# Layer 2's graph attention in one pass over the edges, and linear attention in a phase of its own

## The chip, the cores and the metric

The kernel runs on one core of one Trainium2 chip. Its time is the device time of one execution in microseconds; lower is better. Engines are named as in the profile: PE is TensorE's matrix multiplications and PEld its weight loads, DVE is VectorE, ACT is ScalarE, POOL is GpSimd, SP is SyncE. SPq and ACTq are the queues from which those engines issue transfers.

## What is computed

A graph network with four layers over 3125 nodes of 256 features and 53125 edges, sorted by target. Each layer adds a graph part, a mixing part and a feed-forward part to `x`. The change touches the graph part and the mixing part of layer 2:

```python
# _L2_gnn_ref, 8 heads of 32
h_prime = (x @ W + b).reshape(n, K, F_OUT)
h_src = jnp.sum(h_prime * a_src, axis=2)
h_trg = jnp.sum(h_prime * a_trg, axis=2)
e = jax.nn.leaky_relu(h_src[src] + h_trg[trg], negative_slope=0.2)
e = e - jnp.max(e)                      # one maximum over all edges and heads
exp_e = jnp.exp(e)
denom = jax.ops.segment_sum(exp_e, trg, num_segments=n)
alpha = exp_e / (denom[trg] + 1e-10)
out = jax.ops.segment_sum(h_prime[src] * alpha[:, :, None], trg, num_segments=n)
...
x = x + _L2_gnn_ref(xn, ...) + _L2_mix_ref(xn[None], ...)[0]    # the mixing part is linear attention
```

Each node also has a loop edge to itself, which the kernel handles apart, as `own`.

## The kernel before

The program is a sequence of phases. Each has its own buffers and semaphores and ends with a barrier of all engines. Nodes lie in 25 tiles of 125 rows. Edges are cut into 440 steps of 128 (`STEPS`, `W`), so that all edges of a step have their targets in one tile, whose number stands in `step_tile`; steps with fewer edges are padded. Eight steps are a group (`GROUP`), and there are 55 groups. `StepTiles` loads the tile numbers of a group into registers of an engine.

Layer 2 runs as follows. `project` writes the transformed rows to a table in memory, and `g2_logit` the source logits beside them, 264 columns in all. `start_rows` adds a bias to `x`. Then comes `linear_attention` (phase `m2_att`), with `LogitGather` beside it in the same phase: GpSimd gathers the rows of each step's sources from the table into one of 8 slots (L3562), and SyncE stores the features of each into a second table, `kept2`, and the logits into `alpha` (L3569, L3570). After its own part of the attention, VectorE compares the local target numbers of a group with the partition number (L3590, called `compare` there and `mark` after the change), TensorE multiplies this matrix with the target logits of the step's tile, 8 columns wide, to expand them to the edges (L3603), and ScalarE copies the result (L3613). Each product of a step shows as two entries of PE in the trace.

Phase `g2_exp` adds both logits for all 440 steps at once, applies the leaky ReLU, masks padded edges (`gone`), finds the one maximum by way of a diagonal matrix that TensorE multiplies with ones (the spread), and takes the exponential. Phase `g2_sp` is `weighted_sums`: SyncE loads the stored rows again into 24 slots; for each pair of steps VectorE scales the rows by `alpha` (`scale`, L3204); for each group it makes the matrix of targets (`compare`, L3196, called `match` after the change); TensorE multiplies the two for each step into one of 8 banks (L3188); and VectorE adds the bank to its tile of `total` (`add`, L3211), each add waiting for the one before. `g2_fin` divides by the denominators and adds to `x`, in four passes over all nodes.

Layer 0 has a loop of the same kind (`gathered_sums`, L829 to L877), in which the sums read gathered rows directly.

The order on each engine is the order of the source: nothing is moved by a compiler, and an engine that waits holds up all that stands behind.

## Time and profile before

| | us |
|---|---|
| median of 3 runs (lowest, highest) | 7098.52 (7088.64, 7107.34) |
| the profiled execution | 7097.57 |
| its span in the profile | 7095.8 |
| PE busy | 4572.0 (64%) |
| PEld busy | 3074.1 (43%) |
| DVE busy | 3424.4 (48%) |
| POOL busy | 2538.9 (36%) |
| ACT busy | 1013.3 (14%) |

The span runs from the first to the last instruction of one profiled execution. Busy shares are means over the whole span, in which stages with different limits follow one another. The mean granted clock of TensorE was 0.752 of full speed; 0.50 is its low level, 1.2 GHz, and 1.00 its high one, 2.4 GHz.

### The profile page before, as it was taken

How to read it: one execution, taken by the hardware profiler on the slowest of the kernel's cores; microseconds unless marked ns; L12 is line 12 of the kernel's file. 1: busy time of each engine (PE TensorE's matmuls, PEld its weight loads, DVE VectorE, ACT ScalarE, POOL GpSimd, SP SyncE). 2: the span in 40 equal slices, each digit the busy share in tenths (PEclk: the TensorE clock that was granted, in tenths of full speed). 3: DMA queues.
4: the chain of work that ended last, by engine and by line, in shares of the span. 5: the costliest groups of instructions: out<-in, count | busy, mean ns of one | idle time of the engine just before them, and what ended most of it. 6: DMA issues, size and time to landing. Idle time of an engine off the chain costs nothing. (4 is left out here: it accounts for less than half of the span.)

```text
span 7095.8 us, 70899 instructions
## 1 busy us (share of the span) xinstructions
PE 4572.0 (64%) x17628; PEld 3074.1 (43%) x17628; DVE 3424.4 (48%) x6656; ACT 1013.3 (14%) x2336; POOL 2538.9 (36%) x2523
## 2 busy tenths in 40 slices
PE   0577768876946886564419436834649996777643
PEld 0245533335833332333218323832426774555533
DVE  6234455550035776896631335207972224677622
ACT  0122200012210000110113100001113332111111
POOL 2455567741014775000130327670000003766333
PEclk9877765558976555897659767558979997988766
DMA  2100023340106998442022238884430002322333
GB/s 83 46 2 2 2 76 98 98 119 25 36 27 217 340 339 256 141 149 68 5 90 74 59 99 215 234 218 136 147 95 1 0 0 71 91 82 77 73 86 101
DMA packets 607539, 722.98 MB, mean 102 GB/s; under 512 B 172860, under 2 KB 504495, under 8 KB 606818
## 3 DMA queue, kind: packets, MB, share of 16 engines
q0 software_dynamic: 144448, 324.12, 16.6%
q1 hardware_dynamic: 440918, 356.52, 16.1%
q10 hardware_dynamic: 21854, 38.57, 1.6%
q8 instruction: 140, 2.29, 0.1%
q14 instruction: 179, 1.47, 0.1%
HBM read 532.77 MB, written 184.69 MB: 101 GB/s over the span
## 5 line engine op out<-in xcount | busy, mean ns | idle before, releaser
L829 POOL DMA_INDIRECT m_rows<-support,far_at x440 | 463.8, 1054 | 1400.4 <-POOLq L96 1164.8
L3188 PE MATMUL g_sp_bank<-g_sp_rows,g_sp_same 128*125 128x260 f32 (+1 forms) x1760 | 530.6, 432 | 276.6 <-DVE g_sp_rows L3204 233.9
L840 PE MATMUL g_sums_bank<-g_sums_rows,g_sums_same 128*125 128x256 f32 x880 | 489.7, 667 | 111.1 <-DMA g_sums_rows<-h,far_at 62.8
L487 POOL DMA_INDIRECT records<-record,place_at x416 | 417.7, 1004 | 353.5 <-issue 116.1
L2945 POOL DMA_INDIRECT g_sc_rows<-keyval,src_at x440 | 423.4, 962 | 322.9 <-POOLq L96 172.6
L3188 PEld LDWEIGHTS g_sp_bank<-g_sp_rows,g_sp_same 128*125 128x125 f32 x1760 | 319.3, 200 | 488.2 <-DVE g_sp_rows L3204 339.3
L829 POOL DMA_INDIRECT g_sums_rows<-h,far_at x440 | 455.1, 1034 | 149.6 <-issue 103.7
L3562 POOL DMA_INDIRECT m_att_rows<-h,src_at x440 | 426.4, 969 | 178.9 <-issue 116.6
L2964 PE MATMUL g_sc_pair<-g1q_parts,g_sc_near 125*128 x1320 | 361.8, 411 | 136.0 <-DVE g_sc_rows L3008 106.0
L3211 DVE TENSOR_TENSOR g_total<-g_total,g_sp_bank 125x260 f32 (+1 forms) x880 | 372.9, 424 | 73.9 <-DVE g_total L3211 68.8
L840 PEld LDWEIGHTS g_sums_bank<-g_sums_rows,g_sums_same 128*125 128x125 f32 x880 | 212.5, 298 | 388.0 <-DVE g_total L877 244.0
L877 DVE TENSOR_TENSOR g_total<-g_total,g_sums_bank 125x256 f32 x440 | 185.1, 421 | 289.5 <-PE g_sums_bank L840 286.6
L840 PE MATMUL m_half<-m_rows,m_same 128*125 128x256 f32 x880 | 262.2, 422 | 62.2 <-DVE g_total L877 56.4
L3204 DVE TENSOR_TENSOR g_sp_rows<-g_sp_rows,g_alpha 128x512 f32<-128x512 f32 x440 | 300.9, 684 | 0.1
L877 DVE TENSOR_TENSOR g_total<-g_total,m_half 125x256 f32 x440 | 184.7, 420 | 214.6 <-PE m_half L840 182.1
L1524 DVE SCALAR_TENSOR_TENSOR x<-f_y,f_comb,x 125x256 f32 x200 | 96.8, 484 | 376.0 <-PE f_y L1341 376.0
L1720 POOL DMA_INDIRECT f_back<-answer_rows,f_place_at x100 | 123.5, 1235 | 414.0 <-DMA answer_rows<-f_answer 384.2
L1383 ACT ACTIVATE f_hid<-f_h,f_shift,f_scale 128x375 f32<-128x375 f32 (+1 forms) x320 | 195.6, 612 | 286.2 <-PE f_h L1320 281.0
L2964 PEld LDWEIGHTS g_sc_pair<-g1q_parts,g_sc_near 125*128 125x128 bf16 x1320 | 131.1, 115 | 214.9 <-issue 163.5
L840 PEld LDWEIGHTS m_half<-m_rows,m_same 128*125 128x125 f32 x880 | 160.8, 201 | 140.7 <-DVE g_total L877 113.0
L1712 POOL DMA_INDIRECT sorted_rows<-xn,f_place_at x100 | 125.5, 1255 | 251.5 <-DVE f_place_at L1603 215.2
L3603 PE MATMUL m_att_bank<-g_both,m_att_near 125*128 x880 | 194.1, 360 | 26.8 <-DVE m_att_near L3590 26.3
(639 smaller groups left out, 8668.9 us busy)
## 6 DMA issues: line engine op xcount, KB each, us to landing
g_sp_rows<-kept SPq DMA_DIRECT2D x880, 128.0 KB, 2.1
kept<-g_sc_rows SPq DMA_DIRECT2D x440, 128.0 KB, 15.5
kept<-m_att_rows SPq DMA_DIRECT2D x440, 128.0 KB
xnT<-sorted_rows SPq DMA_DIRECT2D x80, 256.0 KB, 2.9
answer_rows<-f_answer SPq DMA_DIRECT2D x64, 256.0 KB
g_sc_local_in<-local_rows ACTq DMA_DIRECT2D x55, 250.0 KB
m_att_local_in<-local_rows ACTq DMA_DIRECT2D x55, 250.0 KB
sorted_rows<-zero SPq DMA_DIRECT2D x1, 8192.0 KB
```

Of the source, the lines that this page charges most:

```text
L487: nc.gpsimd.indirect_dma_start(core.records, bass.IndirectOffsetOnAxis(ap=core.place_at[:, t:t + 1], axis=0), core.record[:, t, :], None). ...
L829: nc.gpsimd.indirect_dma_start(self.rows[:, k, :], None, self.table, bass.IndirectOffsetOnAxis(ap=core.far_at[:, s:s + 1], axis=0)).then_i ...
L840: nc.tensor.matmul(self.halves[s % slots], self.same[:, g % 2, k, :], self.rows[:, s % self.SLOTS, :], start=True, stop=True).then_inc(sel ...
L877: nc.vector.tensor_tensor(there, there, self.halves[s % len(self.halves)].unsqueeze(1), ALU.add).then_inc(self.added, 1)
L1383: nc.scalar.activation(hid[layer][:, i % 2, mo, 0:n], hbank[q % HR][:, 0:n], func, scale=scale[layer][:, g, mo:mo + 1], bias=shift[layer][ ...
L2945: nc.gpsimd.indirect_dma_start(rows[:, k, :], None, table, bass.IndirectOffsetOnAxis(ap=core.src_at[:, s:s + 1], axis=0)).then_inc(gathere ...
L2964: nc.tensor.matmul(banks[pair % 4][:, s % 2, 0:D], near[:, g % 2, k * W:(k + 1) * W], query[:, i, bass.ds(tile, 1), :].rearrange("p o d -> ...
L3188: nc.tensor.matmul(banks[s % BANKS][0:P, 0:D + heads], same[:, g % 2, k, :], rows[:, s % SLOTS, :], start=True, stop=True).then_inc(summed, 1)
L3204: nc.vector.tensor_tensor(mine, mine, alpha[:, 2 * pair:2 * pair + 2, :].unsqueeze(3).to_broadcast([W, 2, heads, dim]), ALU.mult).then_inc ...
L3211: nc.vector.tensor_tensor(there, there, banks[s % BANKS][0:P, 0:D + heads].unsqueeze(1), ALU.add).then_inc(added, 1)
L3562: nc.gpsimd.indirect_dma_start(self.rows[:, k, :], None, self.table, bass.IndirectOffsetOnAxis(ap=core.src_at[:, s:s + 1], axis=0)).then_i ...
L3603: ins = nc.tensor.matmul(banks[g % 2][:, k * self.heads:(k + 1) * self.heads], self.near[:, g % 2, k * W:(k + 1) * W], self.target[:, bass ...
```

## The change

The gathers, the softmax and the sums of layer 2 become one phase, `attended_sums`, which comes after linear attention; `linear_attention` loses the work beside it. Each edge row is gathered once, into one of 40 slots, and is used there. The maximum over all edges is replaced by a running one: `top[g+1]` is the maximum up to group g. A group's exponentials are taken against it (`grow_act`), and the first add of a group multiplies its tile by `ratio[g]`, the exponential of the maximum before minus the one after. `g2_fin` finds for each tile the maximum up to which it is scaled (`reached`) and takes it to the last one by `factor`. The logits of group g+2 are made while the sums of group g run, and the mark for group g+3. The write to `kept2`, the re-read and the phase `g2_exp` are gone. The leaky ReLU of `own` moves to `g2_logit`. The banks for the sums are 6 in place of 8; the other two hold the expansion and the spread.

```diff
--- before.py
+++ after.py
...
-def linear_attention(core, name, wq, wkv, wo, target, bias=None, clamp=None, plus=None, length=1.0, add=True, beside=None):
+def linear_attention(core, name, wq, wkv, wo, target, bias=None, clamp=None, plus=None, length=1.0, add=True):
...
-class LogitGather:
+class Attend:
+    SLOTS, BANKS = 40, 6
+    LOW = -1e30
+    def __init__(self, core, table, target, heads, total, outer):
+        self.core, self.table, self.target, self.heads, self.total = core, table, target, heads, total
+        self.top, self.minus = outer.sb("top", [W, GROUPS + 1]), outer.sb("minus", [W, GROUPS + 1])
+    def place(self, ph):
+        heads = self.heads
...
+        self.banks = [ph.ps(f"bank{k}") for k in range(self.BANKS)]
+        self.near_bank, self.best_bank = ph.ps("near_bank"), ph.ps("best_bank")
...
+    def gather(self, pool):
+        nc, core = self.core.nc, self.core
+        for s in range(STEPS):
+            k = s % self.SLOTS
+            if s >= self.SLOTS:
+                pool.wait_ge(self.summed, s - self.SLOTS + 1)
+            nc.gpsimd.indirect_dma_start(self.rows[:, k, :], None, self.table,
+                                         bass.IndirectOffsetOnAxis(ap=core.src_at[:, s:s + 1], axis=0)).then_inc(self.gathered[k], 16)
+    def load(self, sp):
+        for g in range(GROUPS):
+            if g >= 2:
+                sp.wait_ge(self.near_set, g - 1)
+            mine = slice(g * GROUP * W, (g + 1) * GROUP * W)
+            sp.dma_start(self.local_in[:, g % 2, :], self.core.local_rows[mine].partition_broadcast(P)).then_inc(self.marked[g % 2], 16)
+    def expand_pe(self, pe, g):
+        nc, heads = self.core.nc, self.heads
+        if g == 0:
+            self.pe_tiles = StepTiles(pe, "expand", self.core.step_tile)
+        self.pe_tiles.load(g)
+        pe.wait_ge(self.near_set, g + 1)
+        if g:
+            pe.wait_ge(self.taken, g)
+        for k in range(GROUP):
+            tile = self.pe_tiles.at(g * GROUP + k)
+            ins = nc.tensor.matmul(self.near_bank[:, k * heads:(k + 1) * heads], self.near[:, g % 2, k * W:(k + 1) * W],
+                                   self.target[:, bass.ds(tile, 1), :].rearrange("p o h -> p (o h)"), start=True, stop=True)
+        ins.then_inc(self.expanded, 1)
+    def spread_pe(self, pe, g):
+        nc = self.core.nc
+        pe.wait_ge(self.diag_set, g + 2)
+        if g >= 0:
+            pe.wait_ge(self.topped, g + 1)
+        nc.tensor.matmul(self.best_bank[:, 0:W], self.ones[:], self.diag[:], start=True, stop=True).then_inc(self.spread, 1)
+    def sum_pe(self, pe, s):
+        nc = self.core.nc
+        g, k = s // GROUP, s % GROUP
+        if k == 0:
+            pe.wait_ge(self.same_set, g + 1)
+        if k % 2 == 0:
+            pe.wait_ge(self.scaled, s // 2 + 1)
+        if s >= self.BANKS:
+            pe.wait_ge(self.added, s - self.BANKS + 1)
+        nc.tensor.matmul(self.banks[s % self.BANKS][0:P, 0:D + self.heads], self.same[:, g % 2, k, :], self.rows[:, s % self.SLOTS, :],
+                         start=True, stop=True).then_inc(self.summed, 1)
+    def grow_act(self, act, g):
+        nc, heads = self.core.nc, self.heads
+        act.wait_ge(self.topped, g + 2)
+        nc.scalar.activation(self.rows[:, self.slots(g), D:D + heads], self.logit[:, g % 2], ACT.Exp, bias=self.minus[:, g + 1:g + 2])
+        nc.scalar.activation(self.ratio[:, g:g + 1], self.top[:, g:g + 1], ACT.Exp, bias=self.minus[:, g + 1:g + 2]).then_inc(self.grown, 1)
+    def begin(self, v, own):
+        nc, core = self.core.nc, self.core
...
+        self.link(nc.vector.memset(self.total[:], 0.0))
+        self.link(nc.vector.tensor_reduce(self.best[0:P, :], own, AX.XY, ALU.max))
...
+        self.tiles = StepTiles(v, "attend", core.step_tile)
+    def mark(self, v, g):
+        nc, core = self.core.nc, self.core
+        v.wait_ge(self.marked[g % 2], 16 * (g // 2 + 1))
+        if g >= 2:
+            v.wait_ge(self.expanded, g - 1)
+        nc.vector.tensor_scalar(self.near[:, g % 2, :], self.local_in[:, g % 2, :], core.row[0:P, 0:1], None, ALU.is_equal).then_inc(self.near_set, 1)
...
+    def logits(self, v, g):
+        nc, core, heads, link = self.core.nc, self.core, self.heads, self.link
+        z = self.logit[:, g % 2]
+        for s in range(g * GROUP, (g + 1) * GROUP):
+            v.wait_ge(self.gathered[s % self.SLOTS], 16 * (s // self.SLOTS + 1))
+        v.wait_ge(self.expanded, g + 1)
+        if g >= 2:
+            v.wait_ge(self.grown, g - 1)
+        nc.vector.tensor_tensor(z, self.rows[:, self.slots(g), D:D + heads], self.near_bank[:, 0:GROUP * heads].rearrange("p (s h) -> p s h", h=heads),
+                                ALU.add).then_inc(self.taken, 1)
+        v.wait_ge(self.taken, g + 1)
+        link(nc.vector.scalar_tensor_tensor(z, z, 0.2, z, ALU.mult, ALU.max))
+        link(nc.vector.tensor_tensor(z, z, bcast_last(self.gone[:, g * GROUP:(g + 1) * GROUP], [W, GROUP, heads]), ALU.add))
+        link(nc.vector.tensor_reduce(self.best[:], z, AX.XY, ALU.max))
+        link(nc.vector.tensor_tensor(self.best[:], self.best[:], self.top[:, g:g + 1], ALU.max))
+        nc.vector.tensor_scalar(self.diag[:], core.ident[:], self.best[:, 0:1], None, ALU.mult).then_inc(self.diag_set, 1)
+    def highest(self, v, g):
+        nc = self.core.nc
+        v.wait_ge(self.spread, g + 2)
+        self.link(nc.vector.tensor_reduce(self.top[:, g + 1:g + 2], self.best_bank[:, 0:W], AX.X, ALU.max))
+        nc.vector.tensor_scalar(self.minus[:, g + 1:g + 2], self.top[:, g + 1:g + 2], -1.0, None, ALU.mult).then_inc(self.topped, 1)
+    def scale(self, v, pair):
+        nc, heads = self.core.nc, self.heads
+        g, k = 2 * pair // GROUP, 2 * pair % self.SLOTS
+        v.wait_ge(self.grown, g + 1)
+        mine = self.rows[:, k:k + 2, 0:D].rearrange("p k (h d) -> p k h d", h=heads)
+        nc.vector.tensor_tensor(mine, mine, self.rows[:, k:k + 2, D:D + heads].unsqueeze(3).to_broadcast([W, 2, heads, D // heads]), ALU.mult).then_inc(self.scaled, 1)
+    def add(self, v, s):
+        nc = self.core.nc
+        g, k = s // GROUP, s % GROUP
+        tile = self.tiles.at(s)
+        v.wait_ge(self.summed, s + 1)
+        if s:
+            v.wait_ge(self.added, s)
+        there, bank = self.total[:, bass.ds(tile, 1), :], self.banks[s % self.BANKS][0:P, 0:D + self.heads].unsqueeze(1)
+        if k:
+            nc.vector.tensor_tensor(there, there, bank, ALU.add).then_inc(self.added, 1)
+        else:
+            nc.vector.scalar_tensor_tensor(there, there, self.ratio[0:P, g:g + 1], bank, ALU.mult, ALU.add).then_inc(self.added, 1)
+def attended_sums(core, attend, own):
+    with Phase(core.nc, "g2_sp") as ph:
+        attend.place(ph)
+        block = ph.block()
...
+        @block.tensor
+        def _(pe):
+            attend.spread_pe(pe, -1)
+            for g in range(2):
+                attend.expand_pe(pe, g)
+                attend.spread_pe(pe, g)
+            attend.expand_pe(pe, 2)
+            for s in range(STEPS):
+                g, k = s // GROUP, s % GROUP
+                attend.sum_pe(pe, s)
+                if k == 5 and g + 2 < GROUPS:
+                    attend.spread_pe(pe, g + 2)
+                if k == 7 and g + 3 < GROUPS:
+                    attend.expand_pe(pe, g + 3)
+        @block.scalar
+        def _(act):
+            for g in range(GROUPS):
+                attend.grow_act(act, g)
+        @block.vector
+        def _(v):
+            attend.begin(v, own[:])
+            for g in range(3):
+                attend.mark(v, g)
+                if g < 2:
+                    attend.logits(v, g)
+                    attend.highest(v, g)
+            attend.match(v, 0)
+            attend.tiles.load(0)
+            for pair in range(GROUP // 2):
+                attend.scale(v, pair)
+            for s in range(STEPS):
+                g, k = s // GROUP, s % GROUP
+                attend.add(v, s)
+                if k % 2 == 0 and g + 1 < GROUPS:
+                    attend.scale(v, (s + GROUP) // 2)
+                if k == 1 and g + 2 < GROUPS:
+                    attend.logits(v, g + 2)
+                if k == 3 and g + 1 < GROUPS:
+                    attend.match(v, g + 1)
+                if k == 5 and g + 2 < GROUPS:
+                    attend.highest(v, g + 2)
+                if k == 6 and g + 3 < GROUPS:
+                    attend.mark(v, g + 3)
+                if k == 6 and g + 1 < GROUPS:
+                    attend.tiles.load(g + 1)
...
 def gnn2_mix2(core):
...
-        alpha = outer.sb("alpha", [W, STEPS, heads])
-        by_dst = outer.sb("by_dst", [W, STEPS, heads])
...
-                nc.vector.tensor_tensor(own[:], both[:, 0], both[:, 1], ALU.add).then_inc(made, 1)
+                link(nc.vector.tensor_tensor(own[:], both[:, 0], both[:, 1], ALU.add))
+                nc.vector.scalar_tensor_tensor(own[:], own[:], 0.2, own[:], ALU.mult, ALU.max).then_inc(made, 1)
         start_rows(core, "m2_start", core.x, None, "L2_mix_bproj")
-        linear_attention(core, "m2_att", "L2_mix_Wq", [("L2_mix_Wkv", None)], "L2_mix_Wproj", core.x, clamp=1e-6,
-                         beside=LogitGather(core, table, kept, alpha, by_dst, both[:, 1], heads))
-        with Phase(nc, "g2_exp") as ph:
...
-        total = outer.sb("total", [P, NT, D + heads])
-        weighted_sums(core, "g2_sp", kept, alpha, heads, total)
...
+                each, each_head = [P, NT, GROUPS], [P, NT, heads]
+                v.wait_ge(tiles_in, 16)
+                link(nc.vector.tensor_copy(first[:], tile_i[:].rearrange("p (g k) -> p g k", k=GROUP)[:, :, 0:1].rearrange("p g o -> p (g o)")))
+                link(nc.vector.tensor_tensor(until[:], bcast_mid(first[:], each), bcast_last(core.ramp[0:P, 0:NT], each), ALU.is_le))
+                link(nc.vector.tensor_scalar(until[:], until[:], 1.0, FAR, ALU.subtract, ALU.mult))
+                link(nc.vector.tensor_tensor(until[:], until[:], bcast_mid(attend.top[0:P, 1:GROUPS + 1], each), ALU.add))
+                nc.vector.tensor_reduce(reached[:], until[:], AX.X, ALU.max).then_inc(reached_set, 1)
+                v.wait_ge(grown, 2)
+                link(nc.vector.tensor_tensor(den[:], total[:, :, D:D + heads], bcast_last(factor[:], each_head), ALU.mult))
+                link(nc.vector.tensor_tensor(den[:], den[:], own[:], ALU.add))
                 link(nc.vector.tensor_scalar(den[:], den[:], 1e-10, None, ALU.add))
                 link(nc.vector.reciprocal(den[:], den[:]))
-                link(nc.vector.tensor_tensor(hd(hprime[:]), hd(hprime[:]), bcast_last(own[:], wide), ALU.mult))
+                link(nc.vector.tensor_tensor(mine[:], den[:], own[:], ALU.mult))
+                link(nc.vector.tensor_tensor(part[:], den[:], bcast_last(factor[:], each_head), ALU.mult))
+                link(nc.vector.tensor_tensor(hd(hprime[:]), hd(hprime[:]), bcast_last(mine[:], wide), ALU.mult))
+                link(nc.vector.tensor_tensor(hd(total[:, :, 0:D]), hd(total[:, :, 0:D]), bcast_last(part[:], wide), ALU.mult))
                 link(nc.vector.tensor_tensor(total[:, :, 0:D], total[:, :, 0:D], hprime[:], ALU.add))
-                link(nc.vector.tensor_tensor(hd(total[:, :, 0:D]), hd(total[:, :, 0:D]), bcast_last(den[:], wide), ALU.mult))
                 link(nc.vector.tensor_tensor(core.x[:], core.x[:], total[:, :, 0:D], ALU.add))
+            @block.scalar
+            def _(act):
+                last = attend.minus[0:P, GROUPS:GROUPS + 1]
+                nc.scalar.activation(own[:], own[:], ACT.Exp, bias=last).then_inc(grown, 1)
+                act.wait_ge(reached_set, 1)
+                nc.scalar.activation(factor[:], reached[:], ACT.Exp, bias=last).then_inc(grown, 1)
```

## Rows read from the trace of the kernel before

**Rows 1.** Windows over layer 2's stretch: busy time, granted clock, DMA.

```profile
4193.00:4206.00 13.00, 0.00 (x0) 0.00 (x0) 0.00 (x0) 0.00 (x0) 7.73 (x9) 0.50 0.68 203
4206.00:4454.10 248.10, 166.06 (x468) 100.90 (x468) 130.80 (x225) 26.07 (x50) 185.53 (x195) 0.78 0.82 214
4454.10:4808.70 354.60, 194.12 (x880) 190.07 (x880) 42.06 (x56) 12.32 (x55) 233.29 (x238) 0.50 0.86 222
4808.70:4834.20 25.50, 1.22 (x2) 0.50 (x2) 19.77 (x14) 3.40 (x2) 0.00 (x0) 0.50 0.00 0
4834.20:5238.00 403.80, 266.59 (x880) 159.72 (x880) 364.31 (x716) 46.33 (x220) 0.00 (x0) 0.94 0.48 144
5238.00:5268.20 30.20, 0.00 (x0) 0.00 (x0) 29.34 (x7) 0.00 (x0) 0.00 (x0) 0.50 0.00 0
```

**Rows 2.** VectorE's timeline in g2_sp: start, length, line, operation.

```profile
5007.21 0.42 DVE L3211 TENSOR_TENSOR g_total<-g_total,g_sp_bank 125x264 f32 x1
5007.55 1.19 DVE L3196 TENSOR_TENSOR g_sp_same<-ramp,local 128x1000 f32<-128x1000 f32 x1
5008.66 0.42 DVE L3211 TENSOR_TENSOR g_total<-g_total,g_sp_bank 125x264 f32 x1
5009.00 0.68 DVE L3204 TENSOR_TENSOR g_sp_rows<-g_sp_rows,g_alpha 128x512 f32<-128x512 f32 x1
5009.60 0.42 DVE L3211 TENSOR_TENSOR g_total<-g_total,g_sp_bank 125x264 f32 x1
5010.23 0.43 DVE L3211 TENSOR_TENSOR g_total<-g_total,g_sp_bank 125x264 f32 x1 [0.21 <-DVE g_total L3211]
```

**Rows 3.** The timeline of two expansions in the attention phase.

```profile
4599.26 0.75 DVE L3590 TENSOR_SCALAR m_att_near<-m_att_local_in,row 125x1024 f32<-125x1024 bf16 x1 [3.27 <-DMA m_att_local_in<-local_rows]
...
4600.16 7.02 PEld L3603 LDWEIGHTS m_att_bank<-g_both,m_att_near 125*128 125x128 f32 x32 [0.54 <-issue]
...
4603.78 0.22 ACT L3613 ACTIVATE g_by_dst<-m_att_bank 128x64 f32<-128x64 f32 x1 [3.80 <-PE m_att_bank L3603]
```

**Rows 4.** Windows over the first two expansions.

```profile
4455.00:4456.60 1.60, 1.52 (x13) 1.53 (x13) 0.56 (x1) 0.00 (x0) 1.30 (x2) 0.94 0.93 229
4456.60:4458.20 1.60, 1.60 (x10) 1.60 (x9) 0.00 (x0) 0.22 (x1) 1.29 (x2) 0.50 0.88 162
```

**Rows 5.** Windows over g2_sp's start and over layer 0's loop.

```profile
4843.20:4848.90 5.70, 5.66 (x13) 4.42 (x14) 5.28 (x11) 0.44 (x3) 0.00 (x0) 0.50 0.88 271
...
943.00:1524.00 581.00, 482.95 (x869) 209.91 (x870) 298.45 (x543) 0.00 (x0) 448.70 (x435) 0.54 0.34 98
```

**Rows 6.** The timeline in layer 0's loop.

```profile
1201.05 0.49 PEld L840 LDWEIGHTS g_sums_bank<-g_sums_rows,g_sums_same 128*125 128x125 f32 x2 [1.57 <-DVE g_total L877]
...
1202.21 0.49 PEld L840 LDWEIGHTS g_sums_bank<-g_sums_rows,g_sums_same 128*125 128x125 f32 x2 [0.67 <-issue]
1202.42 0.42 DVE L877 TENSOR_TENSOR g_total<-g_total,g_sums_bank 125x256 f32 x1 [0.53 <-PE g_sums_bank L840]
```

**Rows 7.** GpSimd's groups by line, from 943 to 1524 and 4680 to 4780.

```profile
L829 POOL DMA_INDIRECT g_sums_rows<-h,far_at x435 | 450.3, 1035 | 132.6 <-issue 102.4 <-PE g_sums_bank L840 30.2
...
L3562 POOL DMA_INDIRECT m_att_rows<-h,src_at x81 | 76.8, 948 | 24.7 <-issue 24.7
```

**Rows 8.** The timeline of linked two-element operations, layer 0.

```profile
672.93 0.16 DVE L2081 TENSOR_TENSOR m_n_stat<-m_n_stat 125x2 f32<-125x2 f32 x1
673.13 0.17 DVE L2082 TENSOR_SCALAR m_n_stat<-m_n_stat 125x2 f32<-125x2 f32 x1
```

**Rows 9.** VectorE's timeline in g2_exp.

```profile
4809.18 3.82 DVE L3677 TENSOR_TENSOR g_alpha<-g_alpha,g_by_dst 128x3520 f32<-128x3520 f32 x1
...
4827.32 0.42 DVE L3687 TENSOR_REDUCE g_exp_top<-g_exp_bank 128x1 f32<-128x256 f32 x1 [1.31 <-PE g_exp_bank L3694]
```

**Rows 10.** The timeline of a small load and its first user.

```profile
4182.35 0.26 SPq L1134 DMA_DIRECT2D m_start_b<-in_L_mix_bproj  x1
4185.51 6.83 DVE L1140 TENSOR_TENSOR x<-x,m_start_b 125x6400 f32<-125x6400 f32 x1 [12.61 <-DMA m_start_b<-in_L_mix_bproj]
```

More of the change, by code:

```diff
@@ L979, in _ @@
             nc.gpsimd.memset(kv[:, :, KV:KV + 1], 1.0).then_inc(ones, 1)
-            if beside:
-                beside.gather(pool)
         @block.tensor
@@ L3592, in expand @@
-    def expand(self, pe, banks):
-        nc, core = self.core.nc, self.core
-        tiles = StepTiles(pe, "expand", core.step_tile)
-        for g in range(GROUPS):
-            tiles.load(g)
-            pe.wait_ge(self.near_set, g + 1)
-            if g >= 2:
-                pe.wait_ge(self.taken, g - 1)
-            for k in range(GROUP):
-                s = g * GROUP + k
-                tile = tiles.at(s)
-                ins = nc.tensor.matmul(banks[g % 2][:, k * self.heads:(k + 1) * self.heads], self.near[:, g % 2, k * W:(k + 1) * W],
-                                       self.target[:, bass.ds(tile, 1), :].rearrange("p o h -> p (o h)"), start=True, stop=True)
-            ins.then_inc(self.expanded, 1)
@@ L3620, in gnn2_mix2 @@
     heads, dim = 8, 32
-    LOW = -1e30
+    FAR = 1e30
     full = D + heads
-    table, kept = core.table("h2", N, full), core.table("kept2", STEPS * W, D)
+    table = core.table("h2", N, full)
     wide = [P, NT, heads, dim]
@@ new lines, in gnn2_mix2, with _ @@
+        attended_sums(core, attend, own)
+        with Phase(nc, "g2_fin") as ph:
+            den, mine, part = ph.sb("den", [P, NT, heads]), ph.sb("mine", [P, NT, heads]), ph.sb("part", [P, NT, heads])
+            tile_i, first = ph.sb("tile_i", [P, STEPS], I32), ph.sb("first", [P, GROUPS])
+            until, reached, factor = ph.sb("until", [P, NT, GROUPS]), ph.sb("reached", [P, NT]), ph.sb("factor", [P, NT])
+            tiles_in, reached_set, grown, chain_sem = ph.sem("tiles_in"), ph.sem("reached_set"), ph.sem("grown"), ph.sem("chain")
+            block = ph.block()
+            @block.sync
+            def _(sp):
+                sp.dma_start(tile_i[:], core.tile_row.partition_broadcast(P)).then_inc(tiles_in, 16)
+                sp.wait_ge(tiles_in, 16)
```

127 lines of the change are left out of this document (37 added, 90 removed).

## The prediction

> **What bounds the kernel now.** I read the page first. No engine is busy for more than 64% of the span (table of the section before), and its chain of work names only a few per cent, so the span is a row of phases with barriers between them, each with a bound of its own; what the change is worth has to be read in layer 2's stretch. I then cut that stretch at its phase borders with the table of windows [rows 1]. Six pieces stand there: linear attention's weight loads (13.0 us), its computation (248.1 us), the rest of that phase, in which only the gathers and the target-logit expansions run (354.6 us), the softmax over all edges `g2_exp` (25.5 us), the weighted sums `g2_sp` (403.8 us), and `g2_fin`. In the third piece GpSimd still issues 238 of its 440 gathers, and VectorE and TensorE end early: it is bound by the gathers. In the fifth VectorE is busy for 364 of 404 us: it is bound by VectorE.
>
> Inside `g2_sp` the timeline of VectorE gives its beat [rows 2]. What counts is the distance between starts: add to match 0.34, match to add 1.11, add to scale 0.34, scale to add 0.60, add to add 0.63 us. The timeline of an expansion gives the other half [rows 3]: the mark (0.75 us on VectorE) ends at 4600.01, TensorE's first load starts 0.15 later, and 32 entries, two groups, take 7.02 us, so 3.5 us a group; ScalarE reads the first of them at 4603.78, 3.6 after the start. That is at a granted clock of 0.50; in the first one, at 0.94, 13 entries took 1.53 us, 0.118 each or 1.9 us a group [rows 4].
>
> **What goes.** All of `g2_exp`, the write and re-read of the gathered rows, and the overlap of gathers with attention. From 4193.0 to 5238.0 the old form takes 1045.0 us [rows 1]; I rebuild this stretch.
>
> **Attention alone.** Its computation stays 248.1 us: no engine there waits for the gathers. Its 1 MB of weights took 13.0 us beside 9 gathers [rows 1]; the lower bound is the 3.2 us of one small load [rows 10]; I take 8, so 256 us.
>
> **The prologue of the new phase.** The second group's logits need 16 gathers. One is issued every (76.8+24.7)/81 = 1.25 us where nothing disturbs it [rows 7], 20 us in all, plus about 3 to land (a load's 3.2 us, [rows 10]). Then logits, spread (a 256-column one kept VectorE 1.31 us, half that width some 0.9, [rows 9]), highest, mark: at 27 us the third expansion starts. It takes 3.5, and the first sum reaches VectorE 1.4 later: 32 us. Bounds 28 and 40.
>
> **One group of the loop.** This decides. In the source TensorE issues `expand_pe(g + 3)` after the sum of k = 7, ahead of all sums of group g+1, and the expansion waits for `mark(g + 3)`, which VectorE reaches only at k = 6 of the same group. The six banks cannot bridge this: TensorE has done, or is about to finish, all eight sums by then, and after the mark VectorE has one add left and then waits for the expansion and the first sum behind it. So mark, expansion and first sum lie one after the other on the path, in 52 of the 55 groups. With t = 0 at the add of k = 0:
> - add 1 waits for its sum: sums at the low clock start 1.16 us apart [rows 6]: t = 1.17.
> - logits: 0.34 to get there; four linked operations on 64 elements, each 0.20 (linked operations on two elements start 0.20 apart, [rows 8]) + 64 × 3.82/3520 [rows 9] = 0.27; one of a single column, 0.20; the diagonal, 0.22 (128 elements, nothing waits for it): 1.50. Ten semaphore waits stand ahead of it, most on their own. No row shows such a row of waits; they cost nothing where they pass under the add before them (0.42), and at most some 1.0 us if each costs 0.1. I take 0.2. Add 2 at 3.21.
> - scale and add 3, 0.94: 4.15. Match and add 4, 0.34 + 1.11: 5.60. Scale and add 5: 6.54. Highest, 0.34 + a reduce of 128 (0.34) + the sign (0.09): add 6 at 7.31. The spread that it reads is issued after the sum of k = 5, which even at the low clock ends at about 6.0: in time. The operand of the spread and the exponentials on ScalarE stay off this path, a group ahead.
> - scale and mark, 0.34 + 0.60 = 8.25; the mark ends at 9.00; TensorE starts at 9.15 [rows 3]; + 3.5 = 12.65; the first sum's load to its add is 1202.42 - 1201.05 = 1.37 [rows 6]: 14.0 us.
>
> **Which clock.** The rows give three cases. Dense wide sums raised it 5.7 us after the first one, in `g2_sp`, and it stayed at 0.94 in the mean with 880 entries in 404 us, 44 in 20 us [rows 1, 5]. In layer 0's loop, of the same sums, TensorE got through 869 entries in 581 us, 30 in 20 us, and the mean was 0.54 [rows 5]. In expansions alone it was 0.50 though the loads kept the engine busy (194 us in 220; the piece is the third of [rows 1]). The new loop has 16 wide entries in 14 us, 23 in 20 us, then, once the clock has risen, 2 us or so of standing and an expansion. So I expect the clock to rise during each run of eight sums, which only takes waiting from a stretch in which VectorE leads, and to be low again for most of the expansion and the first sum. Where it still is high, an expansion takes 1.9 instead of 3.5; I give a fifth of that, 0.3 us: 13.7 us a group, TensorE at about 0.65.
>
> By the Trainium skill, page "TensorE: Matmul & The Clock Gate", section Part 1, activity releases the throttle and the array's busy-ness decides; if the narrow expansions counted as activity, the clock would stay up through them. The trace speaks against it: the expansions of [rows 1] kept their 0.50. What it would give is the second case below.
>
> **GpSimd** is not the bound: undisturbed 1.25 us a gather, 10.0 a group; in layer 0's loop, beside VectorE, (450.3+132.6)/435 = 1.34, 10.7 a group [rows 7]. Both are below 13.7, and 40 slots hold five groups. The row loads of SyncE are issued two groups ahead.
>
> **The end of the loop.** The last three groups have no expansion; by the same distances 8.9, 7.1 and 5.1: 21 us.
>
> **`g2_fin` and the rest.** The four wide passes stay four. New are the load of the step tiles, with nothing beside it (3.0), a small copy (0.3), three operations on 1375 elements at 1.6 and one at 0.9, the exponential with its two handovers (0.5) and three small products (1.2): 10.7 us. The leaky ReLU of `own` adds 0.4 before attention.
>
> **Sum.** 256 + 1 + 32 + 52 × 13.7 (712) + 21 + 1 = 1023 against 1045.0 (+0.5 to the first operation of `g2_fin`), so -22; + 11 gives -11. The profiled execution took 7097.6 us (span 7095.8), the median of the runs is 7098.5, one apart: 7087 us. The gain expected from the removed 25 us, and from 355 us of gathers no longer followed by 404 us of sums, goes into some 4.5 us of idle VectorE per group, and into a VectorE beat of 9 us a group where the sums alone had 7.1.
>
> **The cases.**
> 1. As worked out, 13.3 to 14.2 us a group: 7066 to 7113, middle 7087. Chance 0.5.
> 2. The high clock reaches into or through the expansions. Through all: sums 0.58 apart, expansion 1.9, first sum 0.7, so 9.0 - 0.23 + 0.15 + 1.9 + 0.7 = 11.5 a group and 6973 us; half of it, 12.6, gives 7030. For it: the clock in `g2_sp` fell seldom. Against it: a standing TensorE before every expansion, and 0.50 in all the expansions. Chance 0.2.
> 3. It ends slower: the waits ahead of the logits are paid in full. They stand on VectorE, with add 2 to 7, the mark and so the expansion behind them. At 1.0 more per group, 14.7, it is 7139; at 14.9, 7149. It decides from 14.35 on. For it: nowhere in `g2_sp` does VectorE have more than two waits ahead of an operation, so ten are untried; against it: two pass there with no gap. Chance 0.25.
> 4. GpSimd becomes the bound, because VectorE's two-input work slows the gathers beyond 13.7/8 = 1.71 us each, or its start is late by tens of us: 7120 to 7200. Chance 0.05.
>
> **How the numbers follow.** A measurement of this kernel tells 0.3%, 21 us, from no change. Faster than 7077: the lower fifth of case 1 and case 2, 0.32. Slower than 7120: cases 3 and 4, 0.30. Between: 0.38. The range for 8 in 10 takes case 2 down to 12.4 us a group and case 3 up to 15: 7020 to 7155; case 1 alone is 7066 to 7113.
>
> **What the profile after would show.** Linear attention's phase ends about 256 us after it starts, and the new phase is 765 us long. In it VectorE stands for some 5 us once a group, released by TensorE, between the add of k = 7 and that of k = 0; TensorE stands before each expansion, released by the mark. Gathers run ahead and then wait for sums. Expansions have entries of 0.33 us (low clock) or below 0.2 (case 2). A gap of VectorE ahead of the logits' first operation that ends with "issue" would be case 3. I am wrong altogether if the idle time per group is not there.

## The result and the profile after

The changed kernel takes 7080.9 us (median of 11 runs, 7070.2 to 7091.2), the kernel before 7100.9 us in the runs beside it (7088.6 to 7107.3): a ratio of 0.9972, 95% interval 0.9963 to 0.9982. That is 0.28% less, a real difference, and by the bound of 0.3% that the prediction had set just inside "no change". The forecast was 7087 us; as a gain, 20 us came where 11 had been worked out. The profiled execution has a span of 7078.4 us, 17.4 less than the 7095.8 of before.

The windows of the changed kernel, cut at the borders that the prediction works with (weights of linear attention, its computation, prologue of the new phase, its loop from the first add to the add of step 0 in the last but two groups, the rest, `g2_fin`). Columns as in [rows 1]:

```profile
4192.20:4197.40 5.20, 0.00 (x0) 0.00 (x0) 0.00 (x0) 0.00 (x0) 0.09 (x1) 0.50 0.58 202
4197.40:4445.40 248.00, 167.88 (x468) 101.66 (x468) 129.85 (x223) 26.11 (x50) 0.00 (x0) 0.78 0.00 0
4445.40:4478.80 33.40, 14.38 (x58) 13.05 (x58) 16.66 (x33) 1.07 (x4) 23.89 (x25) 0.55 0.52 132
4478.80:5189.00 710.20, 508.22 (x1771) 417.03 (x1770) 461.18 (x1146) 27.71 (x104) 423.75 (x416) 0.67 0.40 98
5189.00:5209.50 20.50, 13.06 (x46) 7.42 (x45) 17.53 (x41) 0.53 (x2) 0.00 (x0) 0.98 0.00 0
5209.50:5251.00 41.50, 0.00 (x0) 0.00 (x0) 36.20 (x16) 0.78 (x2) 0.00 (x0) 0.51 0.01 5
```

The stretch that took 1045.0 us before [rows 1] takes 1017.3, so 27.7 less, and `g2_fin` 41.5 instead of 30.2. The loop is the piece to look at: 710 us, VectorE busy in 461 of them, TensorE's clock 0.67. One group of it, in the timeline of VectorE, TensorE and its weight loads:

```profile
4806.59 0.49 DVE L3679 SCALAR_TENSOR_TENSOR g_total<-g_total,g_sp_ratio,g_sp_bank 125x264 f32 x1 [4.63 <-PE g_sp_bank L3599]
4807.60 0.42 DVE L3677 TENSOR_TENSOR g_total<-g_total,g_sp_bank 125x264 f32 x1
4807.96 0.22 DVE L3646 TENSOR_TENSOR g_sp_logit<-g_sp_rows,g_sp_near_bank 128x64 f32<-128x64 f32 x1
...
4809.46 0.43 DVE L3677 TENSOR_TENSOR g_total<-g_total,g_sp_bank 125x264 f32 x1
...
4814.68 0.75 DVE L3628 TENSOR_SCALAR g_sp_near<-g_sp_local_in,row 125x1024 f32<-125x1024 bf16 x1
4815.34 0.42 DVE L3677 TENSOR_TENSOR g_total<-g_total,g_sp_bank 125x264 f32 x1
4815.58 3.49 PEld L3579 LDWEIGHTS g_sp_near_bank<-g_both,g_sp_near 125*128 125x128 f32 x16 [4.00 <-issue]
4815.59 3.58 PE L3579 MATMUL g_sp_near_bank<-g_both,g_sp_near 125*128 x16 [3.59 <-DVE g_sp_near L3628]
4818.95 3.18 PEld L3599 LDWEIGHTS g_sp_bank<-g_sp_rows,g_sp_same 128*125 128x125 f32 x8
4820.39 0.49 DVE L3679 SCALAR_TENSOR_TENSOR g_total<-g_total,g_sp_ratio,g_sp_bank 125x264 f32 x1 [4.63 <-PE g_sp_bank L3599]
```

Read it from the mark (L3628). TensorE had stood for 3.6 us and was released by it; VectorE does one more add and then stands for 4.63 us, while the expansion (3.4 us to the first weight load of a sum) and that sum pass. Both engines wait for each other in turn. The waits of the whole loop, in microseconds, times and the longest one, show that this is the pattern of nearly every group and that GpSimd is ahead:

```profile
DVE g_total L3679 <- PE g_sp_bank L3599: 230.9, 53, 5.0
PE g_sp_near_bank L3579 <- DVE g_sp_near L3628: 205.9, 55, 4.7
POOL g_sp_rows L3559 <- PE g_sp_bank L3599: 169.1, 130, 4.3
```

The start of `g2_fin`, where the added work lies:

```profile
5209.15 0.43 DVE L3677 TENSOR_TENSOR g_total<-g_total,g_sp_bank 125x264 f32 x1 [0.21 <-DVE g_total L3677]
5214.05 0.21 DVE L3806 CAST g_fin_first<-g_fin_tile_i 125x55 f32<-125x55 int32 x1 [4.47 <-DMA g_fin_tile_i<-step_tiles]
5214.29 1.59 DVE L3807 TENSOR_TENSOR g_fin_until<-g_fin_first,ramp 125x1375 f32<-125x1375 f32 x1
5215.91 0.88 DVE L3808 TENSOR_SCALAR g_fin_until<-g_fin_until 125x1375 f32<-125x1375 f32 x1
```

### The profile page after: what moved, and what is told of

Its sections match the earlier page's. It is cut to its first block and busy times, and to the rows that moved or that the text cites. A ratio compares the mean times of both kernels' runs of the same rounds, so it can differ in the third digit from the quotient of the medians.

```text
span 7078.4 us, 70101 instructions
## 1 busy us (share of the span) xinstructions
PE 4646.0 (66%) x17738; PEld 3162.7 (45%) x17738; DVE 3501.0 (49%) x7098; ACT 981.6 (14%) x2171; POOL 2554.9 (36%) x2523
## 3 DMA queue, kind: packets, MB, share of 16 engines
q0 software_dynamic: 144448, 324.12, 16.4%
q1 hardware_dynamic: 258118, 253.60, 11.1%
## 5 line engine op out<-in xcount | busy, mean ns | idle before, releaser
L3559 POOL DMA_INDIRECT g_sp_rows<-h,src_at x440 | 447.6, 1017 | 518.6 <-POOLq L96 255.3
L3174 PE MATMUL g_sp_bank<-g_sp_rows,g_sp_same 128*125 128x260 f32 x880 | 264.1, 430 | 135.8 <-DVE g_sp_rows L3190 115.1
L3599 PE MATMUL g_sp_bank<-g_sp_rows,g_sp_same 128*125 128x264 f32 x880 | 348.2, 562 | 4.4 <-DVE g_sp_same L3635 3.1
L3579 PE MATMUL g_sp_near_bank<-g_both,g_sp_near 125*128 x880 | 185.3, 349 | 205.9 <-DVE g_sp_near L3628 205.9
L3579 PEld LDWEIGHTS g_sp_near_bank<-g_both,g_sp_near 125*128 125x128 f32 x880 | 180.3, 312 | 228.2 <-issue 228.2
L3599 PEld LDWEIGHTS g_sp_bank<-g_sp_rows,g_sp_same 128*125 128x125 f32 x880 | 239.9, 286 | 68.0 <-DVE g_sp_same L3635 3.9
L3174 PEld LDWEIGHTS g_sp_bank<-g_sp_rows,g_sp_same 128*125 128x125 f32 x880 | 159.5, 200 | 240.4 <-DVE g_sp_rows L3190 170.0
```

The lines of the kernel that those rows point to most:

```text
L3174: nc.tensor.matmul(banks[s % BANKS][0:P, 0:D + heads], same[:, g % 2, k, :], rows[:, s % SLOTS, :], start=True, stop=True).then_inc(summed, 1)
L3559: nc.gpsimd.indirect_dma_start(self.rows[:, k, :], None, self.table, bass.IndirectOffsetOnAxis(ap=core.src_at[:, s:s + 1], axis=0)).then_i ...
L3579: ins = nc.tensor.matmul(self.near_bank[:, k * heads:(k + 1) * heads], self.near[:, g % 2, k * W:(k + 1) * W], self.target[:, bass.ds(tile ...
L3599: nc.tensor.matmul(self.banks[s % self.BANKS][0:P, 0:D + self.heads], self.same[:, g % 2, k, :], self.rows[:, s % self.SLOTS, :], start=Tr ...
```

## The experiments

Nine runs followed, on three chips. Two of the chips run this program 5 to 6% slower altogether: before took 7481.5 and 7540.8 us there, and with the mark at k = 0 the first add of the loop came at 4737 us of the span where the change had it at 4479. Absolute times are therefore compared within a chip, as ratios to before, and groups across chips by the distance between the adds of step 0 in each trace. I call "the group" the first to the last of these 55 adds divided by 54; it holds the shorter last groups. For the change it is (5204.60 - 4478.81)/54 = 13.44 us. The expectations speak of the 52 full intervals alone, of which the change has 13.64 in the mean; where a forecast is judged, that mean is given too.

**The mark earlier.** VectorE writes the matrix of group g + 3 right after the add and scale of k = 0 instead of after k = 6.

```
                 if k % 2 == 0 and g + 1 < GROUPS:
                     attend.scale(v, (s + GROUP) // 2)
+                if k == 0 and g + 3 < GROUPS:
+                    attend.mark(v, g + 3)
...
-                if k == 6 and g + 3 < GROUPS:
-                    attend.mark(v, g + 3)
```

> The mark for group g+3 moves from k = 6 to k = 0 of group g; nothing else changes, and TensorE still expands after the sum of k = 7. My theory (mark, expansion and first sum lie one after the other) says that TensorE then goes straight from its eighth sum into the expansion: some 7.3 us of sums and spread, 3.5 of expansion, 0.5 of other, 11.3 us a group in place of 13.6, so 7081 - 52 x 2.3 = 6960 us (6940 to 7000), and VectorE's wait at the add of k = 0 shrinks from 4.4 us to below 2. A rival, that VectorE's own work or the gathers set the group, says no change, 7081 us: neither is touched.

Measured: 7269.1 us, ratio 0.9715 (0.9677 to 0.9754), group 11.45 us; over the 52 full intervals (5339.0 - 4737.0)/52 = 11.58, where 11.3 was expected. The chain is broken and 107 us of loop are gone, nearly as forecast; VectorE's wait at the add of k = 0 is 2.3 us in the mean (126 us in 55), not quite below the 2 expected. The adds of step 0 show where the rest is:

```profile
4994.11 0.49 DVE L3679 SCALAR_TENSOR_TENSOR g_total<-g_total,g_sp_ratio,g_sp_bank 125x264 f32 x1 [3.64 <-DMA g_sc_kind_in<-kind_rows]
5004.68 0.49 DVE L3679 SCALAR_TENSOR_TENSOR g_total<-g_total,g_sp_ratio,g_sp_bank 125x264 f32 x1 [1.41 <-PE g_sp_bank L3599]
5017.51 0.49 DVE L3679 SCALAR_TENSOR_TENSOR g_total<-g_total,g_sp_ratio,g_sp_bank 125x264 f32 x1 [3.32 <-DMA g_sc_kind_in<-kind_rows]
```

Groups of 10.57 and 12.83 us alternate. In every second one VectorE waits 3.6 us in the mean (83.2 us in 23 waits) for something that this view can't name (the transfer that it names belongs to a phase long over), and GpSimd resumes 0.11 us after it. What it is comes under "Open" below.

**The mark in the middle,** the same two lines at k = 4.

> As the run before, but the mark moves only from k = 6 to k = 4, which on VectorE's timeline is 1.9 us earlier, later than TensorE's last sum in most groups. My theory: the group is shorter by just that distance, 11.8 us, 7081 - 52 x 1.9 = 6983 us (6970 to 7010), between the change and the mark at k = 0. A rival, that the group is bound by TensorE's total work, says the same time as with the mark at k = 0; one that it is bound by VectorE or the gathers says 7081.

Measured: 7275.9 us, ratio 0.9728 (0.9689 to 0.9766), group 11.66 us; over the 52 full intervals (5336.87 - 4723.72)/52 = 11.79, with 11.8 expected. The wait of VectorE at the add of step 0 fell from 230.9 to 134.7 us. The group is as the theory has it. Between the two places of the mark, though, lie only 0.2 us a group where it says 0.5, and the two times can't be told apart (their intervals overlap): it is the run with the mark at k = 0 that falls short, by its unnamed wait.

**TensorE kept busy ahead of the expansion.** Five products of zeros, 264 columns wide, go into a bank that the next sum overwrites.

```
+    def warm_pe(self, pe, s):
+        pe.wait_ge(self.added, s - self.BANKS + 1)
+        for _ in range(5):
+            self.core.nc.tensor.matmul(self.banks[s % self.BANKS][:, 0:D + self.heads], self.core.zero[:, 0:128],
+                                       self.core.zero[:, 0:D + self.heads], start=True, stop=True)
...
+                    attend.warm_pe(pe, s + 1)
                     attend.expand_pe(pe, g + 3)
```

> Five wide products of zeros (264 columns, the width of a sum) are put between TensorE's eighth sum and its wait for the mark, into the bank that the next sum overwrites; the mark stays at k = 6. They fill most of the 3.7 us in which TensorE stands. My theory of the clock: wide products hold it up, so most expansions run at the high clock (2.0 to 2.3 us in place of 3.5) and the first sum reaches VectorE in 0.8 us in place of 1.4; some 1.6 us less a group on average, 7081 - 83 = 6998 us (6975 to 7035), with a mean clock near 0.95 in the loop. Rival 1, the clock plays no part in the expansion: 7081 us. Rival 2, the extra products end later than the mark and push the expansion back: up to 1 us more a group, 7130 us.

Measured: 7324.1 us, ratio 0.9787 (0.9746 to 0.9829), group 12.70 us, VectorE's wait 191.8 us. Nothing but TensorE's activity differs. The weight loads of the expansion come in two kinds, near 190 and near 333 ns, and what changes is how many there are of each: in the change 81% of the 880 take over 300 ns, here 45%. The median, 333 ns there, is 196 here:

```profile
L3579 PEld LDWEIGHTS g_sp_near_bank<-g_both,g_sp_near x880: 186/196/338, 4680.6 to 5395.7; 125*128 125x128 f32 x176
```

So with products in place of TensorE's standing, fewer of the loads show the low clock, and the group is 0.74 us shorter (0.77 over the 52 full intervals). That is about half of the 1.6 us forecast: the mean granted clock of the loop was 0.78 (0.67 in the change), not near 0.95. Standing right before the expansion isn't all of it either: with the mark at k = 0 TensorE goes from its eighth sum straight into the expansion, and 52% of the loads still take over 300 ns.

**The split alone.** The kernel before, with its gathers and target logits in a phase of their own behind linear attention.

```
-        linear_attention(core, "m2_att", ..., clamp=1e-6,
-                         beside=LogitGather(core, table, kept, alpha, by_dst, both[:, 1], heads))
+        linear_attention(core, "m2_att", ..., clamp=1e-6)
+        with Phase(nc, "g2_lg") as ph:
+            apart = LogitGather(core, table, kept, alpha, by_dst, both[:, 1], heads)
```

> The kernel before with one part of the change alone: the gathers and expansions leave the attention phase and get a phase of their own behind it; softmax over all edges, second table and weighted sums stay. This prices the overlap that the change gives up. Theory: attention alone 253 us, then a phase bound by 440 gathers at 1.25 to 1.30 us, 555 to 575 us, then 25.5 + 404 as before: 1245 us in place of 1045, so 7101 + 200 = 7300 us (7280 to 7325). A rival, that the gathers suffered as much from the attention beside them as the overlap saved, says below 7200.

Measured: 7690.3 us, 208.7 more than before on the same chip, ratio 1.028 (1.0239 to 1.0321). Its windows (attention, gathers, softmax, sums):

```profile
4418.00:4672.00 254.00, 166.14 (x468) 101.14 (x468) 130.19 (x224) 26.11 (x50) 0.11 (x1) 0.77 0.01 4
4672.00:5344.00 672.00, 195.58 (x880) 191.37 (x880) 42.24 (x55) 12.32 (x55) 424.03 (x440) 0.50 0.77 197
5344.00:5369.00 25.00, 0.34 (x1) 0.35 (x2) 16.98 (x11) 0.00 (x0) 0.00 (x0) 0.50 0.18 40
5369.00:5780.00 411.00, 265.58 (x882) 157.77 (x881) 367.13 (x719) 49.71 (x222) 0.00 (x0) 0.94 0.47 141
```

Attention without gathers takes 254 us, as in the change, and nothing in it runs faster for being alone. The overlap that the change gives up was worth 209 us on this chip; the one pass had to earn something like that back before it could gain anything. What it was worth on the first chip no run shows. That 200 had been forecast is in part luck: the phase of the gathers took 672 us, not 555 to 575, so the total can have come out right only because before's own stretch is slower here too. A gather took 672/440 = 1.53 us, not 1.25 to 1.30, because GpSimd also waited for slots to be stored (79.2 us in 65 waits for the store to `alpha` alone). The kernel before shows the same in its third piece: 354.6/238 = 1.49 us a gather [rows 1]. That the piece is bound by gathers, as the prediction reads it, leaves out the stores behind them. TensorE's clock in the second window is 0.50 though its loads keep it busy for 191 of the 299 us that they span: the clock case of the prediction, once more.

**The change again,** as the base of the next three, on one chip.

> The change itself once more, as the base of the three kernels beside it on the same chip. The theory (the order of one group bounds the new loop: mark, weight loads of the expansion at the low clock, first sum, add) expects the same group as on the first chip, 13.6 us, the loop of 52 groups near 710 us, and the add of step 0 waiting 4.4 us a group for the sum. If the chip were what set the group (memory, the gathers), it would differ here.

Measured: 7082.7 us against 7098.8 of before, ratio 0.9974 (0.9963 to 0.9986); group (5212.1 - 4485.5)/54 = 13.46 us, and the add of step 0 waits 232 us in the loop, 4.4 in each of 53 groups. All as expected.

**The expansion in bf16.** The target logits are split into three bf16 parts; VectorE adds them up again.

```
-            ins = nc.tensor.matmul(self.near_bank[:, k * heads:(k + 1) * heads], ...
-                                   self.target[:, bass.ds(tile, 1), :] ...
+            ins = nc.tensor.matmul(self.near_bank[:, k * 3 * heads:(k + 1) * 3 * heads], ...
+                                   self.parts[:, bass.ds(tile, 1), :, :] ...
```

> The expansion's matrices and its target logits in bf16, the logits split in three bf16 parts that are added again after the product, so one pass of 24 columns a step in place of two of 8. The theory (the expansion's 16 weight loads of 0.33 us each at the low clock lie in the chain of the group) expects the expansion at 1.0 to 1.8 us instead of 3.5, a mark of less than 0.75 us, two small operations more on VectorE (+0.5), the group at 11.3 to 12.2 us, and 75 to 120 us less than the change itself on the same chip. The rival (the group is bound by VectorE's own work or by the gathers, or the add waits for something other than the sum, as in every second group of the run with the mark at k = 0) expects less than 40 us.

Measured: 6970.6 us, 112 less than the change, ratio to before 0.9824 (0.9808 to 0.9841), group 11.54 us (11.67 over the full intervals). Time and group lie in the ranges forecast. One expansion and what it releases:

```profile
4808.40 0.48 DVE L3635 TENSOR_SCALAR g_sp_near<-g_sp_local_in,row 125x1024 bf16<-125x1024 bf16 x1
4809.02 1.15 PE L3580 MATMUL g_sp_near_bank<-g_sp_parts,g_sp_near 125*128 x8 [4.40 <-DVE g_sp_near L3635]
4810.07 3.88 PEld L3600 LDWEIGHTS g_sp_bank<-g_sp_rows,g_sp_same 128*125 128x125 f32 x12
4811.48 0.49 DVE L3686 SCALAR_TENSOR_TENSOR g_total<-g_total,g_sp_ratio,g_sp_bank 125x264 f32 x1 [2.26 <-PE g_sp_bank L3600]
```

The chain is the same, each link still there, but 1.05 us stand where 3.4 stood, and the mark takes 0.48 instead of 0.75. VectorE's wait at the add of step 0 fell to 119.2 us.

**Both.** The bf16 expansion and the mark at k = 0.

> The bf16 expansion and the mark at k = 0 together. The theory expects nothing of TensorE left in the chain of the group, VectorE and GpSimd as the bounds: VectorE's work is about 9.8 us, GpSimd's eight gathers 10.0 to 10.8 us, so the group at 10.2 to 11.0 us and 140 to 180 us less than the change itself. With the mark at k = 0 alone the group was 11.45 us, because in every second group the add of step 0 waited 3.6 us more for something that the trace does not name. If that wait belongs to the long fp32 expansion, it is gone here; if not, the group stays at 11.4 us or more, 115 us less than the change itself.

Measured: 6954.8 us, 128 less than the change, ratio 0.9801 (0.9785 to 0.9818), group (5080.7 - 4482.9)/54 = 11.07 us. The gain is less than the 140 to 180 us forecast, the group (11.10 over the full intervals) just above the 10.2 to 11.0. The add of step 0 now waits for 12 us in the whole loop, and the wait without a name is gone. The groups are still uneven: most take 9.5 to 11.1 us, and about every third 13.2 to 14.2. A new wait has come: the logits stand 87.9 us for the landing of their gathers, and GpSimd has no pause but the 0.30 us between two gathers (also where the view puts that pause down to a sum):

```profile
DVE g_sp_logit L3653 <- DMA g_sp_rows<-h,src_at: 87.9, 39, 6.8
L3560 POOL DMA_INDIRECT g_sp_rows<-h,src_at x289 | 312.5, 1081 | 88.1 <-issue 66.7 <-PE g_sp_bank L3600 21.3
```

(312.5 + 88.1)/289 = 1.39 us a gather, 11.1 us for eight: GpSimd sets the group in the mean.

**The first gathers beside attention.** As the run before, with the first 40 gathers issued while GpSimd is idle in linear attention (slots and their semaphores live longer).

```
+            if beside:
+                beside.gather(pool, 0, beside.SLOTS)
+                for k in range(beside.SLOTS):
+                    pool.wait_ge(beside.gathered[k], 16)
...
-            attend.gather(pool)
+            attend.gather(pool, attend.SLOTS, STEPS)
```

> As the run before, with the first 40 gathers issued beside the linear attention, where GpSimd is idle. If GpSimd's row of gathers bounds the loop of the run before, 40 gathers of 1.25 us start 50 us earlier and the whole ends up to 50 us sooner, and the prologue of 33 us falls to about 12; 40 to 60 us less than the run before. If VectorE bounds the loop, only the prologue's part is gained, 20 to 25 us. If neither, nothing.

Measured: 6923.2 us, ratio 0.9753 (0.9737 to 0.9769), 31.6 less than the run before: short of the 40 to 60 that a pure gather bound gives, more than the prologue's share alone. With (5050.1 - 4473.0)/54 = 10.69 us a group the loop gave 21 of them, and its first add came 10 us earlier. Of these the prologue gave only 5.6: from the last add of attention to the first of the loop it takes 26.6 us (32.2 in the run before), not the 12 forecast, because VectorE's own preparation stands there (clearing `total` alone takes 5.56 us); the rest lies ahead of the phase. Until 4641 us VectorE does not wait for gathers at all and a group takes some 9.5 us, VectorE's own beat; then the lead is used up, and it waits about every third group:

```profile
4742.24 0.36 DVE L3657 TENSOR_REDUCE g_sp_logit<-g_sp_near_bank 128x64 f32<-128x192 f32 x1 [4.06 <-DMA g_rows<-h,src_at]
4786.82 0.36 DVE L3657 TENSOR_REDUCE g_sp_logit<-g_sp_near_bank 128x64 f32<-128x192 f32 x1 [4.09 <-DMA g_rows<-h,src_at]
4820.62 0.36 DVE L3657 TENSOR_REDUCE g_sp_logit<-g_sp_near_bank 128x64 f32<-128x192 f32 x1 [4.17 <-DMA g_rows<-h,src_at]
```

The row that the last of these waited for, the 288th gather, was issued at 4815.18 and took GpSimd 1.36 us; it was usable 4 us after that. One thing goes with that. At 4816.14, as soon as the mark has freed the buffer, SyncE issues the 250 KB load of a group's target numbers. By the landing records of the trace, of the 113 gathers of this run that land more than 3 us after GpSimd is done with them, 91 have such a load issued from 2.6 us before to 2.0 us after that moment. The median landing of all gathers beside such a load is 3.2 us, of the others 1.85. The early mark thus issues a load just when the logits of k = 1 need their last row; no run moves the load, so what it costs is not shown. So VectorE bounds the first part and the gathers the rest. This is the fastest of the versions, 2.5% below before and, on this chip, 2.3% below the change (6923.2/7082.7).

**The mark at k = 0 again,** unchanged, because of its unnamed wait.

> The run with the mark at k = 0 alone once more, unchanged, on another chip. On the first chip every second group held a wait of 3.6 us ahead of the add of step 0 that was put down to a transfer, and the group was 11.45 us where the theory gave 10.7. If that wait is the kernel's own, it is here again, in every second group, the group at 11.4 to 11.7 us and the time near 0.984 of before (6985 us where before is 7100). If it was that chip's memory, it is gone, the group is at 10.7 us or less and the time near 0.979 of before.

Measured, on the second slow chip: 7323.7 us, ratio 0.9714 (0.9682 to 0.9745), group 11.59 us. The wait is there again, also in every second group, if not always at the same operation:

```profile
5096.35 0.43 DVE L3677 TENSOR_TENSOR g_total<-g_total,g_sp_bank 125x264 f32 x1 [0.94 <-issue]
5099.25 0.43 DVE L3677 TENSOR_TENSOR g_total<-g_total,g_sp_bank 125x264 f32 x1 [1.87 <-DMA g_sc_kind_in<-kind_rows]
5099.38 0.94 POOL L3559 DMA_INDIRECT g_sp_rows<-h,src_at  x1 [1.96 <-DMA g_sc_kind_in<-kind_rows]
```

It belongs to the kernel, then, not to one chip. (The 10.7 us that the expectation calls the theory's is not what stood in the first one: that was 11.3. Over the 52 full intervals this run has 11.73.) The ratio, far below the expected 0.984, is no sign about the group: the group was as expected, and it is the rest of layer 2 that weighs differently there (below).

## Why the prediction was right

Point by point, by the prediction's own steps:
- **Attention alone:** 253.2 us for weights and computation, predicted 256. The computation was 248.0 (248.1 expected); the weights took 5.2 us where I had taken 8.
- **Prologue:** 33.4 us, predicted 32 and a border of 1.
- **The group:** the 52 intervals of the loop are (5188.27 - 4478.81)/52 = 13.64 us in the mean, predicted 13.7 (709.5 us in all against 712). Its links in the group shown: add 1 at t = 1.01 (predicted 1.17), add 2 at 2.87 (3.21), the mark's end at 8.84 (9.00), TensorE's start at 8.99 (9.15), the first sum's load 3.37 later (3.5), its add 1.44 after that (1.37): 13.80 where the sum without the clock's share had 14.0. Groups in which the clock was still up are the shorter ones: nine of the 52, at 12.4 to 12.8 us, not far from the fifth that the prediction allowed for. Errors of 0.1 to 0.3 in single links partly cancel.
- **The clock:** 0.67 in the loop, about 0.65 predicted. The run with zero products tests the dependence itself: half of the second case was put at 12.6 us a group, and it measured 12.88 over the same 52 intervals. Narrow expansions alone kept 0.50 in the split too, as in [rows 1], with the loads busy for 191 of 299 us. With the rule of the Trainium skill (page "TensorE: Matmul & The Clock Gate", Part 1), that activity releases the throttle, the run with zeros agrees: the mean clock of the loop rose from 0.67 to 0.78.
- **The ten waits ahead of the logits,** the third case: refuted. Add 1 to the logits' first operation is 0.36 us, the same as between an add and what follows it elsewhere [rows 2].
- **GpSimd,** the fourth case: not the bound in the change (it waited 169 us for sums). It became it only at 11.1 us a group, above the 10.7 of [rows 7].
- **The end and `g2_fin`:** 20.5 us for the last groups (21 predicted). `g2_fin` grew by 11.3 us between these windows, 10.7 predicted; VectorE stood for 4.47 us ahead of it, most of it for the step tiles, where before it stood for 0.92, so the load added 3.55 and not 3.0; the three wide operations took 1.59 each as said.
- **Sum:** the stretch fell by 27.7 us (22 predicted); with `g2_fin` that is -16.4 against the -11 worked out, and -17.4 in the spans. The largest single errors are the weights' load, 2.8 us, and the loop, about as much; the medians of all runs lie 20.0 us apart, 2.6 more than the two spans. That total and parts agree so well is in part luck: the links of the group are each off by 0.1 to 0.3 us, in both directions, and 0.1 us a group is 5 us.

That the expected gain was lost in the order of the group, and not in the one pass as such, is shown by runs that each shorten one link or free it. Over the 52 full intervals the mark at k = 4 took off 1.85 us of 1.9 forecast, the mark at k = 0 2.07 of 2.3, and bf16 1.99 where 1.4 to 2.3 was forecast; the clock gave 0.77 of 1.6, the weakest of them. That VectorE's own work or the gathers set the group, the rival of those runs, is refuted by the three that move a mark or a type. That the overlap was worth some 200 us is shown by the split for a slow chip only.

**Open.** Why TensorE's signals come late in every second group with an early mark and an fp32 expansion. That it is they which VectorE and GpSimd wait for, the trace's records of semaphores show, though no view prints them. In the group above, the records put the start of the expansion's last product at 5011.13 us and the first sums from 5011.25 on; but the signal of the expansion stands at 5017.32, and six signals of sums follow within 0.22 us, from 5017.36 to 5017.58. VectorE resumes at 5017.51, GpSimd at 5017.62. In all 55 expansions of the change the signal comes 0.38 us after the start of the last product; with the mark at k = 0 it comes 5.6 to 6.3 us after it in 23 of them and 0.4 us after it in most of the others; with the mark at k = 4 mostly 0.9 to 2.8; in bf16, at either place of the mark, 0.2 (leaving out the few whose own record is missing). So the wait goes with the work on TensorE. Whether the products end late (the profile models their ends) or only their signals come late, these traces don't say. Open is also the size of the change's effect on the two slow chips, where it did not run itself. An estimate: there the mark at k = 0 took 212.4 us off before (7481.5 - 7269.1), and its loop is 107.5 us shorter than that of the change in the result above (54 × 13.44 against 54 × 11.45), so the change would be some 105 us faster, a ratio near 0.986. It would fit that the old form writes and re-reads all rows and the slow chips move less in their busiest slices (below), but no run shows it.

## What to carry to other kernels

When a pass is fused, write down for one round of the new loop which operation of the second engine each engine waits for, and where in the first engine's order that operation is issued. Here one line, the place of the mark, and one data type decided 128 us, several times the 20 that the change brought. And when the chain is broken, work out the beat of every engine anew: the next bound (here GpSimd's gathers at 1.39 us) was only 2.4 us a group away, and part of their cost was then won back by starting them in a phase in which GpSimd stood idle.

## What the runs showed of the hardware

- Ten satisfied semaphore waits ahead of an operation of VectorE cost nothing that the trace shows (0.36 us from add to logits, against 0.34 elsewhere).
- In the split, where TensorE had only products with 8 columns, the granted clock stayed at 0.50 though the loads kept it busy for 191 of 299 us. Ten entries of zeros, 264 columns wide, before each expansion took the share of its loads above 300 ns from 81 to 45% (medians 333 and 196 ns).
- A gather costs 1.39 us a piece beside a VectorE that is busy for 81% of the loop (the run with both), 1.25 where VectorE is idle [rows 7]. Its row is usable 1.85 us after GpSimd is done with it (median), but where the 250 KB load of target numbers is issued beside it 3.2 us (median), in the case shown 4 (4816.54 to 4820.62).
- With fp32 expansions issued straight behind the sums, TensorE's signals came up to 6.3 us after the start that the records give to the product (0.38 us in the change).
- Chips differ by 5 to 6% on this program. Some 258 of the 383 us lie ahead of the new loop; the busiest stretch of transfers there moved 268 to 269 GB/s in its slices where the profile of the change above has 339 to 341.
